# Attention with values of two key tiles in one TensorE block: one core, two-layer gated cross-attention

## The reference

```python
x = x + tanh(g_xattn[0]) * L0_xattn(layernorm(x), ctx, ctx, ...)          # 16 heads of 16, causal
x = x + tanh(g_ffn[0])   * L0_ffn(layernorm(x), ...)                      # 8 experts, top 2
x = x + tanh(g_xattn[1]) * L1_xattn(layernorm(x), ctx, ctx, ..., mask)    # 16 heads of 16, mask
x = x + tanh(g_ffn[1])   * L1_ffn(layernorm(x), ...)                      # 16 experts, top 2, and a shared one

# of both attentions
q, k, v = queries @ Wq.T + bq, keys @ Wk.T + bk, values @ Wv.T + bv       # split into 16 heads
attn = softmax(q @ k.T / sqrt(16) + mask) @ v
out = attn @ Wo.T + bo
```

## Time and profile before

| | |
|---|---|
| median of three runs | 1653.33 us |
| span of the profiled execution | 1659.2 us |
| PE busy | 1465.2 us (88%) |
| DVE (VectorE) busy | 876.3 us (53%) |
| ACT (ScalarE) busy | 678.8 us (41%) |
| POOL (GpSimd) busy | 409.0 us (25%) |
| attention of layer 0, from the first maxima piece to the last value matmul | 73.5 to 535 us |
| attention of layer 1, the same | 1108 to 1299.9 us |

### The profile page before, as it was taken

One profiled execution on the slowest core, in us unless ns is written; L12 is line 12 of the kernel. 1 busy time (PEld: TensorE's weight loads), 2 busy tenths in 40 slices (PEclk: granted clock), 3 DMA queues, 4 the chain that ended last, 5 costly groups with the idle time before them and its releaser, 6 DMA issues. The chain is left out here.

```text
span 1659.2 us, 25681 instructions
## 1 busy us (share of the span) xinstructions
PE 1465.2 (88%) x8638; PEld 880.1 (53%) x8640; DVE 876.3 (53%) x2046; ACT 678.8 (41%) x1108; POOL 409.0 (25%) x346
## 2 busy tenths in 40 slices
PE   5688999989899857999999999469999766999996
PEld 3443433323232636999999999312333442666664
DVE  5689898887870673222222232688887364211110
ACT  4124556756678221333332333216778331022222
POOL 0200000099920062111111111020000316036554
PEclk9779999999999988999999999769999978999998
DMA  5900505127305542137814131340100401246553
GB/s 178 271 5 28 154 20 169 41 80 227 113 1 154 201 178 87 26 101 195 202 22 106 22 108 19 92 129 20 40 21 2 140 18 48 68 113 151 133 135 48
DMA packets 104050, 160.39 MB, mean 97 GB/s; under 512 B 15624, under 2 KB 85276, under 8 KB 101791
## 3 DMA queue, kind: packets, MB, share of 16 engines
q1 hardware_dynamic: 68319, 100.46, 19.9%
q0 software_dynamic: 22528, 48.87, 12.2%
q10 hardware_dynamic: 13120, 10.01, 2.2%
HBM read 101.76 MB, written 58.20 MB: 96 GB/s over the span
## 5 line engine op out<-in xcount | busy, mean ns | idle before, releaser
L813 DVE TENSOR_REDUCE mxp<-psA 128x1 f32<-128x384 f32 (+4 forms) x640 | 335.2, 578 | 65.3 <-PE psA L669 50.8
L787 ACT ACTIVATE Pt<-psC 128x1024 f32<-128x1024 f32 (+4 forms) x296 | 256.3, 918 | 166.7 <-PE psC L695 89.2
L669 PE MATMUL psA<-Kst,Qst 97*128 97x512 bf16 (+5 forms) x896 | 268.0, 366 | 56.5 <-DVE mxp L813 27.6
L669 PEld LDWEIGHTS psA<-Kst,Qst 97*128 97x128 bf16 x896 | 77.3, 100 | 276.4 <-DVE mxp L813 140.3
L695 PE MATMUL psC<-Qst,Kst 100*128 100x512 bf16 (+4 forms) x848 | 220.6, 369 | 3.0 <-DMA Qst<-mT 1.9
L1754 PE MATMUL psA<-xTt,OT 128*128 128x128 f32 x1728 | 203.2, 278 | 4.6 <-issue 4.5
L1754 PEld LDWEIGHTS psA<-xTt,OT 128*128 128x128 f32 x1728 | 198.4, 194 | 10.6 <-issue 10.6
L813 DVE TENSOR_REDUCE mxpt<-psA 128x1 f32<-128x449 f32 x256 | 145.2, 620 | 26.5 <-PE psA L669 21.5
L1841 DVE SCALAR_TENSOR_TENSOR Qst<-psA,b,sil 128x128 f32<-128x128 f32 x216 | 64.3, 346 | 153.0 <-ACT sil L1815 153.0
L787 ACT ACTIVATE Ptt<-psC 128x1024 f32<-128x1024 f32 (+1 forms) x128 | 123.8, 1020 | 47.7 <-PE psC L695 47.3
L718 PE MATMUL psO<-Pt,Vaug 128*17 128x512 f32 (+4 forms) x1184 | 142.6, 553 | 0.0
(11 more groups left out here) (328 smaller groups left out, 1802.9 us busy)
## 6 DMA issues: line engine op xcount, KB each, us to landing
rows<-blank SPq DMA_DIRECT2D x4, 4386.0 KB, 17.2
OT<-L_w SPq DMA_DIRECT2D x8, 2048.0 KB
mi<-mask POOLq DMA_DIRECT2D x16, 800.5 KB, 4.7
Qst<-q_parts SPq DMA_DIRECT2D x96, 128.0 KB, 2.8
Kst<-k_parts SPq DMA_DIRECT2D x12, 800.5 KB, 15.5
w<-L_w SPq DMA_DIRECT2D x8, 1024.0 KB
wg<-L_w_gate POOLq DMA_DIRECT2D x16, 352.0 KB
wu<-L_w_up POOLq DMA_DIRECT2D x16, 352.0 KB
```

Of the source, the lines that this page charges most:

```text
L669: mmi = pe.matmul(out, Qst[0:KA, half[u] % QN, at:at + P], Kst[0:KA, h, k0:k0 + w], start=True, stop=diag is None and not masked)
L787: act.activation(Pt[0:kw, n % SLOTS, :, col:QC], psC[0:kw, n % 2, :].rearrange("p (y t) -> p y t", y=2)[:, :, col:QC], ACT.Exp).then_inc(p ...
L813: dve.tensor_reduce(mxp[:, q, h, pc:pc + 1], psA[:, place_of[("piece", n)] % AB, 0:w], AX.X, ALU.max).then_inc(a_free, 1)
```

## The change

Values of two key tiles are taken in one block in the versions without a mask operand (`together = 2`); in the version with one it stays at one tile. `SLOTS` becomes `2 * together + 2`, 6 slots where it was 4. `values_after[i]` names the steps whose values are taken in the step after i: for 4, 8 and 12 tiles all are pairs, for 13 tiles tile 0 stands alone. The maxima pieces of a step are placed anew: in a step without values half of them stand between the two score packs, in a step with values a quarter between the packs, a quarter between the second pack and the values; the rest comes at the end as before. The number of pieces of each step, all shapes and all other engines' work stay.

```diff
-SLOTS = 4
...
+            together = 1 if masked else 2
+            SLOTS = 2 * together + 2
+            values_after = {}
+            for i, (u, _, j) in enumerate(STEPS):
+                n_tiles = TILES[UNITS[u][0]]
+                if (n_tiles - 1 - j) % together == 0:
+                    values_after[i] = range(i - min(together - 1, j), i + 1)
+
...
+            def cuts(i, n):
+                m = upto[i] - n
+                if i - 1 not in values_after:
+                    return n + m // 2, n + m // 2
+                return n + (m + 1) // 4, n + (m + 1) // 4 * 2
+
             for i in range(len(STEPS)):
-                middle = (n + upto[i]) // 2
+                middle = cuts(i, n)[1]
                 USERS += [("piece", n) for n in range(n, middle)]
...
                 for i in range(len(STEPS)):
-                    for b in range(2):
-                        score_pack(i, b)
-                    middle = (n + upto[i]) // 2
-                    for n in range(n, middle):
+                    early, middle = cuts(i, n)
+                    score_pack(i, 0)
+                    for n in range(n, early):
                         max_piece(n)
-                    if i:
+                    score_pack(i, 1)
+                    for n in range(early, middle):
+                        max_piece(n)
+                    for v in values_after.get(i - 1, ()):
                         for b in range(2):
-                            value_pack(i - 1, b)
+                            value_pack(v, b)
                     if i in turn_at:
                         turn_maxima(turn_at[i])
                     for n in range(middle, upto[i]):
                         max_piece(n)
                     n = upto[i]
-                for b in range(2):
-                    value_pack(len(STEPS) - 1, b)
+                for v in values_after[len(STEPS) - 1]:
+                    for b in range(2):
+                        value_pack(v, b)
```

## The result

The changed kernel takes 1697.95 us (median of four runs, 1695.57 to 1699.51), the kernel before 1651.82 in the same comparison: a ratio of 1.0278, 95% interval 1.0261 to 1.0295. It is slower by 46.1 us, where 32.8 were forecast (1686), inside the range.

What follows compares the result with a forecast made beforehand. The prediction took PE to set the step in most steps, VectorE in layer 0's five-piece steps and ScalarE where there are no pieces. Its terms summed to 32.8 us more: 1653.3 + 32.8 = 1686, range 1662 to 1701.

Steps and rivals of the forecast that it cites:

- step (b): PE's two-step period with double blocks, walked through: waits for psA banks and an exponential, +0.17 us a pair in layer 1.
- (a): Value blocks on PE: 104 fewer, each saving 0.20 us of entry and exit, 21 us if PE only streamed.
- The doubt of 9 us: Other end of the double block's length, 1.87 us or 0.09 more: 104 x 0.09 = 9 us, for the range.
- PE's waits for reductions: Sign in the new profile: PE's weight loads and matmuls wait several tens of us longer in all.
- (c): Sums over both layers by kind of step (pieces per step): 32.8 us more, of which four pieces in layer 0 7.9.
- (f): Unit ends, VectorE held during GpSimd's mask work: three holds, 10.8 us together; no change expected, +-7 for the range.
- (d): Maxima pieces between the score packs: help only against the double block's waits, nothing with single blocks; cost 0.
- (e): Six slots: an exponential waits for the value block three steps back instead of two, always over by then; cost 0.
- Rival 1: Faster: PE's drain decides, banks never run out; 1632.5 us, or 1641 with no-piece steps losing 9; chance 0.08.
- Rival 2: About even: layer 1 and layer 0's four-piece steps gain half the drain, others lose; 1653 to 1665; chance 0.10.

Runs made afterwards that it cites:

- run 9: The change with half reductions and half exponentials together, so another output: 1601.83 us (one execution).
- run 6: The change with each maxima reduction over half of its columns: 1642.37 us, 22.0 over the kernel before with the same half reductions.
- run 8: The change with each exponential over half of its columns, so another output: 1665.22 us (one execution).
- run 1: The kernel before, unchanged, for a second profile: 1654.00 us, spanning 1652.0.
- run 11: The change with four probability slots instead of six: 1717.79 us (one execution).
- run 3: The change with both score packs ahead of the pieces, as in the kernel before: 1702.90 us.
- run 4: The change with single value blocks in the head groups whose steps have no pieces: 1688.07 us.
- run 10: The change with ScalarE's read-out of psO one step later where the next group has an even number of tiles: 1698.10 us against 1697.95.
- run 2: The change with single value blocks and four slots, pieces still between the packs: 1653.54 us against 1651.87 for the kernel before.
- run 12: The kernel before with six slots and nothing else: 1652.65 us against 1650.91.

## Why the prediction was right, and where it was not

**Direction and periods.** The walk of step (b) gave 5.61 us for two steps with four pieces in layer 1; it is 5.59. It gave 5.02 with no pieces; it is 5.01 to 5.02. It gave 5.38 with three; it is 5.39 where no transposes fall, and 5.46 to 5.98 around them. It gave 5.50 with four in layer 0; it is 5.45 to 5.52. Durations of separate instructions from the trace of before, put into the new order with its waits, were enough.

**(a) The block.** 0.20 a pair was forecast as what is saved; run 9 shows 0.22. A double block lasts 1.84, not 1.87. The doubt of 9 us over its length is gone: it was never longer. The Trainium skill's rule on mode changes, that TensorE is drained by one (TensorEngine Tiling (Array Packing), Key Properties), agrees with these 0.22 us; what would follow from it alone, 21 us less, did not come, for what stands outside of PE. That the 0.22 are a drain is not shown: the blocks also go from bfloat16 to float32 operands and back, and no run separates the two.

**(b) The cause was named wrong in most steps, though the sum was right.** The walk lists three waits, 0.05 and 0.25 for banks and 0.05 for an exponential, and the prediction adds them up. They are not additive: the pack at 3.02 is set by a chain of its own, from the first pack after the block (0.39) through two exponentials (0.64 + 0.92 + 1.02) and the release (0.05). Without any wait for a bank it would start at the same time. Run 6 shows that: with reductions at 388 ns the period stays at 5.59. Even run 8, with the exponentials halved, falls only to 5.54, because the bank waits are the next limit right beneath. Both must go before 5.21 comes out. The same is true of four pieces in layer 0 (halves: 5.52 to 5.35; banks: no change) and of three in layer 1 (5.39 to 4.83 by exponentials alone). Only the five- and eight-piece steps are held by the banks alone, as forecast. A sign that the prediction named says the same by failing. PE's waits for reductions ahead of pieces were to grow by several tens of us; they fell, from 233.2 us in 347 waits (run 1; 242.6 in the first profile) to 221.2 in 461, weight loads and matmuls together. What grew were the waits for exponentials ahead of score packs, from 27.6 us in 47 waits to 54.6 in 106. (A weight load can wait while matmuls still run, so these sums are not PE's losses.)

**(c) Sizes.** Seven of the eight terms are within 1.4 us. The eighth, four pieces in layer 0, was 7.9 and measured 14.6. Its steady pairs are as forecast: 0.2 on 41 pairs is 8.2. The rest sits in two kinds of places. At the three unit ends that fall into GpSimd's work VectorE was held 12.4 us in after against 7.8 in run 1, 4.6 more:

```profile
365.86 2.86 DVE L844 TENSOR_TENSOR mparts<-zero,mx 128x16 bf16<-128x16 f32 x1
...
369.17 3.75 DVE L847 TENSOR_TENSOR mparts<-mx,mparts 128x16 bf16<-128x16 f32 x1
```

And at a unit end without any GpSimd work beside it, in the head group of steps 60 to 71, 3.7 us are lost where the group before it loses 0.9. There VectorE splits the maxima undisturbed (0.19 us an operation), and PE, just out of a double block, waits 1.69 us for a bank (0.64 at the same piece in run 1). After that TensorE's granted clock is at its lower level, 1.2 GHz, for some 3 us (the 0.50 in the second view below), and the next double block takes 2.10 to the next matmul instead of 1.84:

```profile
322.18 0.31 PE L683 MATMUL psA<-Kst,Qst 97*128 97x321 bf16 x1 [1.69 <-DVE mxp L830]
...
325.29 2.16 PE L732 MATMUL psO<-Pt,Vaug 128*17 128x512 f32 x16
327.39 0.47 PE L683 MATMUL psA<-Kst,Qst 97*128 97x384 bf16 x2
```

```profile
322.50:325.80 3.30, 3.30 (x15) 1.23 (x16) 2.04 (x5) 1.75 (x2) 0.00 (x0) 0.50 0.00 0
```

The pair of steps 68 and 69 takes 7.62 us there (5.74 in run 1). In runs 8 and 11, with double blocks too, PE waits the same 1.69, but the clock does not fall, and the pair takes 6.02 and 6.04: some 1.6 us are the clock's, and the wait alone does not tell whether it falls. It also falls in steps with five pieces, from 192.8 to 196.1 us (0.50), after PE has stood still 1.03 us where it stood 0.41 in run 1; that pair takes 8.22 us where it took 6.04, 2.2 of the 9.0 us of its row. Every profile with double blocks and full reductions (after, runs 3, 4, 8, 10, 11) has this second fall, and none with single blocks has either. So a part of what the double block costs is a lower clock behind a longer wait of PE.

The terms that were mis-sized are thus (f), for which nothing was put into the sum, and the ordinary unit ends, which have no term at all. For (f) the profile of before had not 10.8 us of holds, as the prediction says, but 13.5: two of 1.37 and 1.38 at 404.79 and 449.29 were not counted. Against its own span the sum gave 1659.2 + 32.8 = 1692.0, and after spans 1696.5, 4.5 us more; against the median it fell 12 short (1686 and 1697.95). Whether the new order meets GpSimd's work more often on average stays open: the medians differ by 46.1, the spans by 37.3 or 44.5, depending on which profile of before is taken. Profiles of the old order have 13.5, 7.8, 8.4 and 7.9 us of holds (before, runs 1, 2, 12), those of the new one or nearly so 12.4, 13.0, 9.6, 11.6 and 8.7 (after, runs 10, 3, 4, 11). And (c) has 2.0 for the eight-piece steps without a walk behind it; they took 3.6.

**(d), (e)** Pieces between the packs: 1.7 us lost with single blocks (run 2), 5 us saved with double ones (run 3), both near the noise. Slots: nothing with single blocks (run 12), 20 us with double ones (run 11). Both had been costed at zero for the right reason, as cover for the double block's own damage.

**The rivals.** Rival 1 (the drain decides, 1632 to 1641) needed banks that never run out; with banks that come back in 388 ns (run 6) the double block still costs 22 us, so what refuses it as well is the mechanism it did not name, the two halves of psC. Rival 2 (half of the drain gained in the four-piece steps) hung on the bank wait of 0.25, which run 6 removed without effect.

## What to carry to other kernels

Longer blocks of one kind on the engine that sets the pace save a fixed cost per switch, here 0.22 us, and take it from the engines around it in idle time: look at the block's length beside what the buffers toward each consumer hold (here 1.84 us against three reductions, 1.62, and two exponentials, 1.94), not at the consumer's share of busy time. That comparison alone does not decide: 1.84 is under 1.94, and yet the exponentials set most periods. Walk one period through with each wait written as a maximum, and look for the longest chain; waits along different chains must not be added, and the limit right beneath the first tells what removing it would bring. Before trusting one profiled execution as the base of a sum, compare its time with the median; a contention that comes by chance (VectorE held under GpSimd's work) can be worth as much as a term. And look at the granted clock wherever a wait of the pacing engine has grown: here two stretches of it at the lower level came with the longer blocks.

## What was not expected of the hardware

Reductions over half the columns in the kernel before brought 32 us (1620.36): the kernel is far more bound by its maxima than the windows' busy shares (87.02 of 95 us at most) had told. It is not a version to use: it leaves half of the columns out of the maxima.

An operation of VectorE of 0.17 us was held for up to 3.78 us beside one of GpSimd. The held ones here all read two tensors: additions and subtractions (L827, L829, L830 and their successors) and in runs 10 and 12 the scaled subtraction between them (L847 and L828, 3.69 and 3.20 us). The Trainium skill, SBUF — State Buffer, SBUF: two separate sides, describes an exclusive lock on a port pair that both engines share, held for a whole instruction; a row of run 1 agrees with that (3.21 held beside a GpSimd operation of 3.21, L1317). Beside GpSimd's L1315, of 4.28 us, it is not as plain: one operation was held 3.75 us, to 0.96 before that one's end by the profile, whose spans of GpSimd are rough, and two in its last 0.31 us (349.90 and 350.11 in run 1) took their usual 0.17.
